# Weights ring and attention rows shifted by 32 bytes in the on-chip buffer

## The reference

```python
def bi_wkv(r, k, v, w, u, time_emb):          # forward and backward decaying sums over time
    a, b = a * decay + exp(k) * v, b * decay + exp(k)      # a scan over 512 positions, both ways
    return sigmoid(r) * (num / max(den, 1e-8)) * (0.8 + 0.2 * tf)

x = x + attention(bi_wkv(x, f, f, w1, u1, cond), Wq, Wk, Wv, Wo, betas)   # 16 heads of 128
x = x + ffn(bi_wkv(x, f, f, w2, u2, cond), W1, W2, W3)                    # 2048 hidden
```

## Time and profile before

| | us |
|---|---|
| median of three runs | 1709.46 |
| the profiled execution, its own time | 1711.2 |
| its span, first to last instruction | 1709.3 |
| TensorE busy in the span | 1583.7 (93%) |
| VectorE busy | 1148.5 (67%) |
| ScalarE busy | 736.5 (43%) |
| GpSimd busy | 563.1 (33%) |

### The profile page before, as it was taken

The page is one execution under the profiler, slowest core; times in us unless marked ns, Lnnn a source line. Parts: engine busy times, 40 slices in busy tenths (PEclk is TensorE's granted clock), DMA queues, the critical chain, the costliest instruction groups (busy, mean ns, idle before and its releaser), DMA issues.

```text
span 1709.3 us, 26926 instructions
## 1 busy us (share of the span) xinstructions
PE 1583.7 (93%) x9696; PEld 1413.8 (83%) x9696; DVE 1148.5 (67%) x2680; ACT 736.5 (43%) x1611; POOL 563.1 (33%) x410
## 2 busy tenths in 40 slices
PE   1479988999999999999999999878799999999999
PEld 0379977998999999999999999767588888888887
DVE  8768966887788787887754764553787885333333
ACT  2246735534644544644534543641454442222221
POOL 5465576121232113121000100232655553443331
PEclk9789998999999999999999999989899999999999
DMA  3185676576466357454565465346222212311101
GB/s 114 56 297 181 210 277 241 176 250 246 151 210 208 137 209 260 138 201 164 202 208 218 166 252 199 116 159 234 87 62 75 62 50 93 117 44 56 46 17 49
DMA packets 112452, 266.49 MB, mean 156 GB/s; under 512 B 11281, under 2 KB 36289, under 8 KB 111681
## 3 DMA queue, kind: packets, MB, share of 16 engines
q1 hardware_dynamic: 93744, 237.51, 39.6%
q10 hardware_dynamic: 18576, 27.27, 5.4%
HBM read 216.48 MB, written 48.25 MB: 155 GB/s over the span
## 4 chain that ended last, share of the span: by engine, by line
PE 83%; DVE 5%; DMA 4%; issue 3%; ACT 2%; SPq 1%; POOL 1%; ACTq 0%; DVEq 0%; POOLq 0%
PE psG L459 16%; PE psG L461 15%; PE psG L460 15%; PE psX L460 3%; PE psX L459 3%; PE psX L461 3%; PE psX L614 3%; PE psX L567 3%; PE psZ L595 2%; PE psZ L586 2%; PE psY L461 2%; PE psY L459 2%; PE psY L460 2%; PE psZ L461 2%; PE psZ L459 2%
## 5 line engine op out<-in xcount | busy, mean ns | idle before, releaser
L459 PE MATMUL psG<-yh,wh 128*128 128x512 f32 x632 | 261.2, 413 | 38.1 <-DVE sg L1008 19.3
L1564 POOL TENSOR_TENSOR wl<-stage,wh 128x512 fp32r<-128x512 f32 x160 | 230.7, 1466 | 175.2 <-ACT wh L1194 173.9
L461 PE MATMUL psG<-yh,wl 128*128 128x512 f32 x632 | 250.2, 396 | 0.0
L460 PE MATMUL psG<-yl,wh 128*128 128x512 f32 x632 | 250.1, 396 | 0.0
L1627 POOL TENSOR_TENSOR vs<-v,omb 128x512 f32<-128x512 f32 x64 | 96.1, 1523 | 375.2 <-PE psX L614 371.0
L459 PE MATMUL psG<-wh,yh 128*128 128x256 f32 x512 | 152.4, 298 | 44.1 <-POOL yl L1589 44.1
L459 PEld LDWEIGHTS psG<-yh,wh 128*128 128x128 f32 x632 | 122.0, 193 | 60.2 <-issue 19.9
L1634 POOL TENSOR_TENSOR hl<-sg,hh 128x512 fp32r<-128x512 f32 x64 | 86.5, 1351 | 225.2 <-ACT hh L1406 225.2
L459 PE MATMUL psG<-ah,wh 128*128 128x256 f32 x512 | 146.7, 287 | 3.5 <-POOL wl L1564 3.5
L461 PE MATMUL psG<-wh,yl 128*128 128x256 f32 x512 | 145.7, 285 | 0.0
L460 PE MATMUL psG<-wl,yh 128*128 128x256 f32 x512 | 145.6, 284 | 0.0
(11 more groups left out here) (188 smaller groups left out, 4193.1 us busy)
## 6 DMA issues: line engine op xcount, KB each, us to landing
wh<-high_o SPq DMA_DIRECT2D x56, 512.0 KB, 3.8
wl<-low_o SPq DMA_DIRECT2D x56, 512.0 KB, 4.8
stage<-in_w SPq DMA_DIRECT2D x64, 256.0 KB, 3.1
wh<-high_v SPq DMA_DIRECT2D x24, 512.0 KB, 4.0
wl<-low_v SPq DMA_DIRECT2D x24, 512.0 KB, 5.3
wh<-high_k SPq DMA_DIRECT2D x24, 512.0 KB, 4.2
wl<-low_k SPq DMA_DIRECT2D x24, 512.0 KB, 5.6
wh<-high_q SPq DMA_DIRECT2D x24, 512.0 KB, 4.5
```

What stands on the lines that cost most here:

```text
L459: e.matmul(out, lh, rh, start=first, stop=False, skip_group_check=check)
L460: e.matmul(out, lh, rl, start=False, stop=False, skip_group_check=check)
L461: return e.matmul(out, ll, rh, start=False, stop=last, skip_group_check=check)
L1564: e.tensor_tensor(lo, raw, hi, ALU.subtract).then_inc(p_wl, 1)
```

## The change

Five unused tensors are put between others. One of 32 bytes ahead of `wh` moves the ring's twelve slots to 32 bytes beyond a multiple of 64; one behind `wl` brings `stage` and all after it back to multiples of 64. The same is done around `ah` and `al`. A pad of 64 bytes ahead of `x` moves the feed-forward's tensors along with the attention's, over which they lie. No instruction is added, removed or moved in order, and sizes, access patterns and semaphores stay; what differs is start addresses. By the sizes in the code `wh` and `wl` move by 32 bytes, `stage` to `xb` by 64, `ah` and `al` by 96, `qT` and all behind it and `x` and all behind it by 128.

```diff
         yh = [sb(ctx, f"yh{i}", [P, NC, T], F32R) for i in range(2)]
         yl = [sb(ctx, f"yl{i}", [P, NC, T], F32R) for i in range(2)]
+        sb(ctx, "pad3", [P, 8])
         wh = [sb(ctx, f"wh{i}", [P, 1024], F32R) for i in range(NRING)]
         wl = [sb(ctx, f"wl{i}", [P, 1024], F32R) for i in range(NRING)]
+        sb(ctx, "pad4", [P, 8])
         stage = [sb(ctx, f"stage{i}", [P, 512]) for i in range(NSTAGE)]
...
         one = ExitStack()
         xb = sb(one, "xb", [P, NC, T])
+        sb(one, "pad5", [P, 8])
         ah = sb(one, "ah", [P, 16, 256], F32R)
         al = sb(one, "al", [P, 16, 256], F32R)
+        sb(one, "pad6", [P, 8])
         qT = sb(one, "qT", [P, 2, T])
...
         one.close()
 
+        sb(ctx, "pad7", [P, 16])
 
         x = sb(ctx, "x", [P, 2, NC, T])
         zh2 = sb(ctx, "zh2", [P, NC, T], F32R)
```

## The result

| | before | after |
|---|---|---|
| median, us | 1709.6 (5 runs, 1708.51 to 1710.48) | 1725.27 (5 runs, 1723.48 to 1727.73) |
| ratio, 95% interval | | 1.0092 (1.0077 to 1.0107) |
| profiled execution: own time, span, us | 1711.2, 1709.3 | 1727.73, 1725.9 |

The change makes the kernel 0.9% slower: 15.7 us in the medians, 16.6 in the spans. The likeliest case, no change, did not come true. The time lies inside the range 1704 to 1732, but by luck: none of the rivals that made the range so wide is its cause.

A forecast was written before the change was run, and what follows sets the result against it. TensorE, busy 93% of the span, was taken as the bound: matmuls times start-to-start distance. All terms were 0 (0 + 0 + 0 + 0), giving 1709.5 us, own range 1706 to 1713, wider range 1704 to 1732.

The forecast's parts named there:

- The likeliest case, no change: Whole kernel: forecast 1709.5 us, with differences up to about 0.2% (3.4 us) counted as no change; chance 0.57.
- the range 1704 to 1732: Whole kernel, us: meant to hold the forecast and the slower prices of A and B; 0.18 left out.
- The frame: TensorE bounds: time is matmuls times start-to-start distance; 6912 matmuls touch moved tensors, 1239 us of the 1709.
- the value 0 for TensorE's reads: Stream and weight loads: 0 us taken; the surplus, 13.3 ns per matmul beyond its columns, was not tied to addresses.
- 213 ns of stream to hide behind: Weight loads with 512 columns: each load has 213 ns of stream to hide behind, against 107 ns in `wo`.
- worth less than 1 in 884: Feed-forward halves: a 256-byte step between operands matters less than this, as both do 884 matmuls in 200 us.
- A: Rival, v and `wo`: moving operand needs one more 64-byte piece, 127 ns a matmul; +20.5 us, 1730; chance 0.14.
- B: Rival, `wo` only: longer weight load, 133 ns a matmul; +20.5 us, 1730; chance 0.06.
- C: Rival, ring DMAs: slower packets; 1712 us at 6%, about 1775 if their time doubled; chance 0.06.
- D: Rival, faster: TensorE's two reads collide, moving them apart helps 5376 matmuls, not `wo`; 1674 or 1638 us; chance 0.13.
- E: Rival, whole kernel: allocator rounds pads to 64, nothing moves; time 1709.5 us; chance 0.57 together with the forecast.
- Other engines, DMAs and pads at 0: ScalarE, GpSimd, VectorE 0 (-1.6 to +1.6 us); DMAs 0 (bound +2 us); pads add no instruction, 0 us.

The follow-up runs named there:

- m2_map: Kernel of matmuls alone: 64 pairs of operand starts 0 to 112 bytes, then one operand moved up to 16 KB; 24 matmuls took 5.55 to 5.71 us in the groups quoted.
- ring_64: Against the kernel before: only the ring (wh, wl) 64 bytes on, other tensors keeping their places within 256 bytes; 1721.01 us, ratio 1.0059.
- heads_only: Against the kernel before: pads only around ah and al and before x, so ah and al are 32 bytes off, the ring stays; 1710.28 us, ratio 1.0004.
- m1_phases: Kernel of matmuls alone, 48 per kind; stationary starts sta to stf: 0, 16, 32, 48, 64, 128 bytes; moving mva to mvd: 0 to 48; (mva,stc) took 233.1 ns each.
- all_32: Against the kernel before: one 32-byte pad ahead of the first tensor moves all tensors together; 1709.32 us, ratio 0.9991.
- heads_192: Against the kernel before: only ah and al moved 192 bytes modulo 256, all others by multiples of 256; 1702.92 us, ratio 0.9968.
- m3_map: Kernel of matmuls alone, all 256 pairs of stationary (s) and moving (m) starts in 16-byte steps, d = s less m; settled 226.7 to 236.7 ns at 512 columns.

## Why the prediction was wrong

- **The frame was right.** The time is a number of matmuls times their distance; 6912 of them touch a moved tensor; only the distances moved.
- **The step that failed** is the value 0 for TensorE's reads ("nothing in the rows ties the surplus to an address"). For the 3840 matmuls of 512 columns with the ring stationary the surplus of 13.3 ns grew to 20.0 in the feed-forward. I bounded the stream where an operand *moves* and the load where it is *as long as the stream*, and gave no upper bound at all to 512 columns, which had "213 ns of stream to hide behind". That was the largest population and it carries +22.7 us of the account.
- **The inference behind it** was the earlier trace rows: `yh` and `zh2` lie 256 bytes apart and cost the same, so distance is "worth less than 1 in 884". The row is right, the reading is not. m2_map shows that 256 bytes is the period, so the row compared a place with itself. ring_64 is the test that the trace of before did not hold.
- **A** (an extra piece in v and `wo`, 127 ns) is wrong in sign: 117.8. **B** (133 ns in `wo`) also. Their price, 20.5 us, put the range's upper end at 1732, and the time fell inside for another reason, by luck.
- **C**: not seen. Landings of 3.7 and 4.8 us, q1 at 39.1% where it had 39.6%. Its upper price was added up wrongly: 37 and 34 us on 1709.5 are 1780, not 1775.
- **D** had the right place: two operands of TensorE, costly or cheap by their distance, seen only at full clock. Its sign was wrong for 512 columns as they lie here: together they are cheap, apart dear. For 256 columns it is right: at d = 4 `wo` has 113.5 ns in ring_64, half of the surplus gone. I had given it 0.13, and it deserved its mirror image as a rival on the slow side.
- **E**: refuted; the pads moved what they should.
- **Other engines, DMAs and pads at 0**: right, within 2 ns on each of the three lines and 0.1 us on the landings of the earlier trace rows (0.3 on the slowest group of loads, 5.9 to 6.2 us). The 14 instructions of line 1562 went from 879 to 937 ns, 0.8 us in all, but to 938 in heads_only too, where the ring stands still.
- The rule weighed from the Trainium skill, page "SBUF — State Buffer", section "SBUF: two separate sides" (reads in lines of 16 bytes), gave 0 for a move by whole lines. m1_phases has operands whole lines apart at 226.9 (mva,stf) and at 233.1 ns (mva,stc), so for TensorE's pair of reads the measurement decides against it. The splitting of transfers by the Trainium skill, page "DMA: Bandwidth & Descriptors", section "How a descriptor splits into AXI transactions", would have added 2 us by the prediction's estimate. No run shows it: all_32, with the whole ring 32 bytes off, took 1709.32 us against 1710.41.

## What to carry to other kernels

Where TensorE is the bound and every float32r matmul loads its own weights, the place of the stationary operand relative to the moving one, modulo 256 bytes, is a knob, worth 1.5% here between the slowest and the fastest placing. With the moving operand at an even multiple of 16 bytes the lowest were the same place for 512 columns and the stationary 64 bytes ahead for 256; at an odd multiple, 192 bytes ahead (32 and 96 also) for 512 columns and 64 for 256. Alignment to 64 bytes of each tensor by itself says nothing. When such a pace is measured, the first dozen matmuls should be left out, and an average should be looked at for two levels. And before a row "that did not care about a step" is used to say that steps are free, ask whether the step might be a whole period; such a test needs at least two unequal sizes.

## What was not expected of the hardware

- A stream of float32r matmuls of 512 columns with a weight load each settled at 226.7 to 236.7 ns apiece at the granted clock 1.00 in m3_map, by the two places; one of 256 columns at 113.3 to 120.3, with one pair at 123.3. At the clock 0.50 the two placings that differ by 6.7 ns took 427 ns each.
- The pace settles only after up to a dozen matmuls, and the same places can settle on two levels (113.3 and 117.8 ns in heads_192). Why is open.
- That the stationary operand's place changes the pace of the stream (m2_map, moving operand fixed) is more than I had thought possible. The Trainium skill, page "TensorE: Matmul & The Clock Gate", section "Step-by-step: what each phase is for", has two independent read ports of which the one for weights takes nothing from the other. The rows do not show ports, but they do show 5 ns (5.55 against 5.67 us for 24) that hang on the stationary operand's address.
- It is not monotonic: with the stationary operand 16 bytes ahead 512 columns settle at 226.7 to 236.7 ns, and at 236.7, the worst of all, in five of the eight pairs with an odd m.
